# Cross-attention and mixture-of-experts kernel: VectorE subtracts the score maxima of two of four units, and every engine's calls stand in a new order

## The reference

```python
x = x + xattn(layernorm(x), ctx, ctx)     # 8 heads of width 16
x = x + moe(layernorm(x))                 # 8 experts, top 2, hidden width 256
# xattn: q, k, v = projections; scores = q k^T / 4
#        attn = softmax(scores, axis=1)   # axis 1 is the HEAD axis
#        out = (attn v) W_O
# moe:   gates = softmax of the two largest router logits, 0 elsewhere
#        out = sum_e gates_e * (relu(x W1_e + b1_e) W2_e + b2_e)
```

## Time and profile before

| | |
|---|---|
| median of three runs | 210.16 us |
| span of the profiled execution | 207.8 us |
| instructions | 4986 |
| TensorE, VectorE busy | 199.5 us, 167.8 us |
| ScalarE, GpSimd busy | 132.2 us, 112.3 us |

### The profile page before, as it was taken

The page is one execution under the profiler, slowest core; times in us unless marked ns, Lnnn a source line. Parts: engine busy times, 40 slices in busy tenths (PEclk is TensorE's granted clock), DMA queues, the critical chain, the costliest instruction groups (busy, mean ns, idle before and its releaser), DMA issues.

```text
span 207.8 us, 4986 instructions
## 1 busy us (share of the span) xinstructions
PE 199.5 (96%) x1752; PEld 176.5 (85%) x1752; DVE 167.8 (81%) x453; ACT 132.2 (64%) x316; POOL 112.3 (54%) x132
## 2 busy tenths in 40 slices
PE   6999988798999999999999999999999999999995
PEld 6845976686799979997999799998998899789994
DVE  6398769889789999899788988898999888556633
ACT  2236748697568847797677767677757776345441
POOL 8502647869976378629561966376746674010000
PEclk9999999999999999999999999999999999999999
DMA  6649595716515133423140504241000000000000
GB/s 175 160 127 286 153 279 148 224 46 183 158 62 145 69 108 106 103 76 104 41 147 25 170 3 151 57 144 36 0 0 28 0 2 3 25 3 2 25 3 25
DMA packets 20264, 18.70 MB, mean 90 GB/s; under 512 B 1776, under 2 KB 18704, under 8 KB 20240
## 3 DMA queue, kind: packets, MB, share of 16 engines
q1 hardware_dynamic: 17344, 16.85, 28.0%
q10 hardware_dynamic: 2896, 1.54, 2.8%
HBM read 11.83 MB, written 6.55 MB: 88 GB/s over the span
## 4 chain that ended last, share of the span: by engine, by line
PE 91%; DVE 3%; ACT 2%; issue 1%; POOL 1%; POOLq 0%; ACTq 0%; DVEq 0%
PE y_ps L436 28%; PE h_ps L421 22%; PE score_ps L361 7%; PE misc_ps L380 6%; PE score_ps L349 6%; PE h_ps L369 4%; PE score_ps L277 3%; PE misc_ps L401 2%; PE score_ps L338 2%; PE score_ps L421 2%; PE misc_ps L389 2%; PE misc_ps L287 1%; PE misc_ps L327 1%; PE misc_ps L306 1%; PE misc_ps L300 1%
## 5 line engine op out<-in xcount | busy, mean ns | idle before, releaser
L695 ACT ACTIVATE hT<-h_ps,b_sb 128x256 f32<-128x256 f32 x118 | 49.4, 470 | 33.3 <-PE h_ps L421 32.1
L436 PE MATMUL y_ps<-w_sb,hT 128*128 128x128 f32 x508 | 68.0, 277 | 0.0
L436 PEld LDWEIGHTS y_ps<-w_sb,hT 128*128 128x128 f32 x508 | 62.8, 191 | 3.5 <-issue 2.2
L1188 POOL TENSOR_TENSOR half_sum<-e_sb 128x512 f32<-128x512 f32 x28 | 37.3, 1332 | 30.8 <-ACT e_sb L667 30.5
L938 DVE TENSOR_TENSOR attn<-e_sb,e_rcp 128x1024 f32<-128x1024 f32 x32 | 42.1, 1319 | 3.3 <-ACT e_rcp L678 3.3
L930 DVE TENSOR_REDUCE shift_m<-score_ps 128x128 fp32r<-128x1024 f32 x32 | 38.7, 1212 | 2.2 <-PE score_ps L338 1.1
L421 PE MATMUL h_ps<-x1T_hi,w_lo 128*128 128x256 f32 x118 | 37.7, 320 | 1.5 <-ACT hT L695 0.9
L667 ACT ACTIVATE e_sb<-score_ps 128x1024 f32<-128x1024 f32 x32 | 32.8, 1024 | 5.6 <-PE score_ps L361 5.4
L1007 DVE SCALAR_TENSOR_TENSOR acc<-y_ps,gates,acc 128x128 f32<-128x128 f32 x96 | 29.0, 342 | 8.6 <-PE y_ps L436 7.3
L421 PE MATMUL h_ps<-x1T_hi,w_hi 128*128 128x256 f32 x118 | 33.1, 280 | 0.0
L421 PE MATMUL h_ps<-x1T_lo,w_hi 128*128 128x256 f32 x118 | 33.1, 280 | 0.0
(11 more groups left out here) (117 smaller groups left out, 291.3 us busy)
## 6 DMA issues: line engine op xcount, KB each, us to landing
k_scratch<-k_parts SPq DMA_DIRECT2D x14, 256.0 KB, 2.6
k_stack<-k_scratch SPq DMA_DIRECT2D x14, 256.0 KB, 4.0
q_stack<-q_scratch SPq DMA_DIRECT2D x28, 128.0 KB, 2.7
q_scratch<-q_parts SPq DMA_DIRECT2D x7, 256.0 KB, 2.7
w_sb<-in_w SPq DMA_DIRECT2D x1, 1024.0 KB, 6.6
out_y<-y_out SPq DMA_DIRECT2D x7, 128.0 KB, 1.9
x_all<-in_x ACTq DMA_DIRECT2D x1, 768.0 KB, 6.2
ctxT<-in_ctx_t SPq DMA_DIRECT2D x1, 640.0 KB, 6.1
```

Source lines behind the costliest of these rows:

```text
L436: mm = nc.tensor.matmul(product(j, t), hT[:, j % 2, c, t * P:(t + 1) * P], w2_sb[:, e * HC + c, :], start=(c == 0), stop=(c == HC - 1))
L695: op = nc.scalar.activation(hT[:, j % 2, c, :], hidden(j)[:, c * S:(c + 1) * S], ACT.Relu, bias=b1_sb[:, e * HC + c:e * HC + c + 1])
L1188: nc.gpsimd.tensor_tensor(half_sum[:], e[:, 0:HQ // 2], e[:, HQ // 2:HQ], ALU.add).then_inc(sum_step, 1)
```

## The change

From batch 1 on, units 2 and 3 are no longer shifted on TensorE. Behind its maximum VectorE subtracts it from the scores, from PSUM into `e_sb`, and ScalarE takes the exponential of `e_sb` in place. The scores' bank is still released by the exponential. All periods are unrolled, and each engine has one list of calls in an order of its own. The diff is cut here to the new step and to the parts of the order that the prediction speaks of.

```diff
+    VECTOR_UNITS = (2,3,)
+    FIRST_VECTOR = 1
...
+        def vector_shifts(n):
+            return n >= UNITS * FIRST_VECTOR and n % UNITS in VECTOR_UNITS
+
+        def shifts_on_vector(n):
+            return sum(vector_shifts(k) for k in range(n))
...
             def subtract_max(b, u):
+                if vector_shifts(UNITS * b + u):
+                    return
...
             def exponentiate(b, u):
                 n = UNITS * b + u
-                act.wait_ge(shifted, n + 1)
+                if vector_shifts(n):
+                    act.wait_ge(vector_shifted, shifts_on_vector(n + 1))
+                    nc.scalar.activation(e_sb[:, u, :], e_sb[:, u, :], ACT.Exp, scale=SCALE).then_inc(exp_made, 1)
+                    return
+                act.wait_ge(shifted, n + 1 - shifts_on_vector(n))
...
             def head_max(b, u):
...
+                n = UNITS * b + u
+                if vector_shifts(n):
+                    dve.wait_ge(max_made, n + 1)
+                    wait(dve, attn_made, n - 3)
+                    nc.vector.tensor_tensor(e_sb[:, u, :].rearrange("p (h q) -> p h q", h=H),
+                                            score_ps[:, u % 2, :].rearrange("p (h q) -> p h q", h=H),
+                                            shift_m[:, u % 2, :].bitcast(F32).unsqueeze(1).to_broadcast([P, H, P]),
+                                            ALU.subtract).then_inc(vector_shifted, 1)
```

The start of SyncE's queue, as calls. Before: `x(0)`, `ctxT(0)`, `spill_k(1)`, `load w1`, `load_k_stack(1)`, `spill_q(1)`, `load_q_stack(1)`, `spill_k(2)`, `load ctxT(3..7)`, `load_k_stack(2)`, `spill_q(2)`, `load_q_stack(2)`, `load w2`. After:

```diff
+            load_first()
+            load_w1()
             spill_k(1)
             load_k_stack(1)
+            load_ctx_rest()
             spill_q(1)
+            spill_k(2)
+            spill_q(2)
+            load_k_stack(2)
+            load_w2()
+            load_q_stack(2)
             load_q_stack(1)
```

On ScalarE's queue the loads were w_qkvo, x(1), ctxT(1), ctxT(2), the rest of x, the small ones, and then `take_k_first`. After:

```diff
+            load_w_qkvo()
+            load_tables()
+            load_x1()
+            load_ctx(2)
+            load_small()
+            take_k_first()
+            load_ctx(1)
+            take_xnT(0)
+            take_k_hi(1)
+            load_x_rest()
+            split_w1(0)
+            split_w1(1)
+            exponentiate(0, 0)
+            exponentiate(0, 1)
+            take_k_hi(2)
+            invert_sum(0, 0)
+            take_xnT(1)
+            make_xn(2)
+            make_xn(3)
+            invert_sum(0, 1)
+            take_q_hi(1)
+            take_xnT(2)
+            exponentiate(0, 2)
+            exponentiate(0, 3)
+            invert_sum(0, 2)
+            take_q_hi(2)
```

TensorE's start after (before, `project_v(0)` stood second, `project_q(0)` ahead of `project_k(1)`, `project_q(1)` ahead of `subtract_max(0, 1)`, and head sums and scores of batch 1 alternated):

```diff
+            keep_warm(12)
+            project_k(0, None, 0)
+            keep_warm(5)
+            transpose_xn(0, None, 0)
+            keep_warm(1)
+            project_k(1, k_first_made, 1)
+            keep_warm(2)
+            project_q(0, xnT_taken, 1)
+            first_scores(0)
+            first_scores(1)
+            project_k(2, None, 0)
+            transpose_xn(1, q_wide_made, 2)
+            subtract_max(0, 0)
+            head_sum(0, 0, k_lo_made, 1)
+            subtract_max(0, 1)
+            first_scores(2)
+            first_scores(3)
+            head_sum(0, 1, log_made, 1)
+            subtract_max(0, 2)
+            project_q(1, xnT_taken, 2)
+            subtract_max(0, 3)
+            transpose_xn(2, k_lo_made, 2)
+            head_sum(0, 2, log_made, 2)
+            project_q(2, xnT_taken, 3)
+            scores(1, 0)
+            scores(1, 1)
+            project_v(0, None, 0)
+            head_sum(0, 3, log_made, 3)
+            attend_values(0, q_lo_made, 2)
```

VectorE's start after:

```diff
             ln1(0, TT, 0)
             ln1_end(0, 0)
+            ln1(2, 4, 1)
+            negate_ident()
+            k_lo(1)
+            mark_heads()
+            split_wr()
+            spread_q(0)
+            spread_q(1)
+            head_max(0, 0)
+            head_max(0, 1)
+            ln1_end(1, 1)
+            ln1(4, 6, 2)
+            ln1(6, 10, 3)
+            head_max(0, 2)
+            head_max(0, 3)
+            k_lo(2)
+            normalize(0, 0)
+            normalize(0, 1)
+            q_lo(1)
+            ln1(10, 16, 4)
+            normalize(0, 2)
+            q_lo(2)
+            head_max(1, 0)
+            head_max(1, 1)
+            normalize(0, 3)
+            add_residual(0)
```

More of the change, by code:

```diff
@@ L441, in expert_down @@
                     mm.then_inc(y_done, 1)
[L443 to L503, removed]
@@ new lines, in _ @@
+            route(0, x1T_lo_made, 1)
+            expert_up(0, 0)
+            scores(2, 0)
+            expert_up(0, 1)
+            subtract_max(1, 3)
+            expert_up(0, 2)
+            expert_down(0, 0)
+            project_k(3, logits_made, 1)
+            scores(2, 1)
+            subtract_max(2, 0)
+            expert_down(0, 1)
+            transpose_xn(3, k_lo_made, 3)
+            expert_up(0, 3)
+            expert_down(0, 2)
+            project_q(3, xnT_taken, 4)
+            expert_up(0, 4)
@@ new lines, in _ @@
+            subtract_max(2, 1)
+            scores(2, 2)
+            attend_values(1, q_lo_made, 3)
+            gated_b2(0, heads_taken, 2)
+            scores(2, 3)
+            subtract_max(2, 2)
+            expert_up(0, 5)
+            expert_down(0, 3)
+            project_out(1, b2_added, 1)
+            expert_up(0, 6)
+            project_k(4, x1_made, 2)
+            expert_down(0, 4)
+            expert_down(0, 5)
+            transpose_x1n(1, k_lo_made, 4)
+            scores(3, 0)
@@ new lines, in _ @@
+            subtract_max(2, 3)
+            expert_down(0, 6)
+            expert_up(0, 7)
+            route(1, x1T_lo_made, 2)
+            expert_up(1, 0)
+            expert_down(0, 7)
+            transpose_xn(4, logits_made, 2)
+            expert_up(1, 1)
+            project_v(3, xnT_taken, 5)
+            scores(3, 1)
+            subtract_max(3, 0)
+            project_q(4, v_taken, 4)
+            expert_up(1, 2)
+            expert_down(1, 0)
+            project_v(4, q_lo_made, 4)
@@ new lines, in _ @@
+            subtract_max(3, 1)
+            scores(3, 2)
+            attend_values(2, v_taken, 5)
+            expert_up(1, 3)
+            project_out(2, heads_taken, 3)
+            expert_down(1, 1)
+            expert_down(1, 2)
+            scores(3, 3)
+            expert_up(1, 4)
+            project_k(5, x1_made, 3)
+            subtract_max(3, 2)
+            expert_down(1, 3)
+            expert_up(1, 5)
+            gated_b2(1, k_lo_made, 5)
+            expert_down(1, 4)
+            transpose_xn(5, b2_added, 2)
@@ new lines, in _ @@
+            expert_up(1, 6)
+            subtract_max(3, 3)
+            scores(4, 0)
+            transpose_x1n(2, xnT_taken, 6)
+            expert_down(1, 5)
+            expert_up(1, 7)
+            subtract_max(4, 0)
+            route(2, x1T_lo_made, 3)
+            expert_down(1, 6)
+            scores(4, 1)
+            expert_up(2, 0)
+            project_q(5, logits_made, 3)
+            expert_down(1, 7)
+            scores(4, 2)
+            subtract_max(4, 1)
+            project_v(5, q_lo_made, 5)
@@ new lines, in _ @@
+            subtract_max(5, 1)
+            project_v(6, q_lo_made, 6)
+            expert_up(3, 2)
+            attend_values(4, v_taken, 7)
+            expert_down(3, 1)
+            project_out(4, heads_taken, 5)
+            scores(5, 2)
+            subtract_max(5, 2)
+            expert_up(3, 3)
+            project_k(7, x1_made, 5)
+            expert_down(3, 2)
+            scores(5, 3)
+            expert_up(3, 4)
+            gated_b2(3, k_lo_made, 7)
+            expert_down(3, 3)
+            expert_up(3, 5)
@@ new lines, in _ @@
+            expert_down(4, 0)
+            project_v(7, q_lo_made, 7)
+            expert_up(4, 2)
+            scores(6, 2)
+            attend_values(5, v_taken, 8)
+            subtract_max(6, 1)
+            expert_up(4, 3)
+            expert_down(4, 1)
+            subtract_max(6, 2)
+            scores(6, 3)
+            expert_down(4, 2)
+            expert_up(4, 4)
+            project_out(5, heads_taken, 6)
+            expert_down(4, 3)
+            expert_down(4, 4)
+            expert_up(4, 5)
```

1136 lines of the change are left out of this document (658 added, 478 removed).

## The result

The changed kernel takes **339.53 us** (median of 4 runs, 336.51 to 342.87), the kernel before 209.83 us on the same chip (4 runs, 209.46 to 210.30). The ratio is 1.6139, with a 95% interval of 1.6051 to 1.6227. The forecast was 240 us, with a range of 226 to 248: the sign was right, and the loss is 129.7 us where some 30 were foreseen. The longest run, 342.87, counts as a slow one, and the ratio is that of the fast runs; the other three have a median of 338.42.

The account below looks back on a forecast made before the run. TensorE bounds the old kernel, VectorE the new middle. Residual at 52.4 + 147.8 work + 4 waits = 204.2; + 0.1 + 30.9 + 2.1 = span 237.3; with 2.4 from span to median, 240 us, range 226 to 248.

Parts of the forecast that it names:

- The bound of the kernel before: Steady middle: TensorE sets the pace, busy all 22.00 us per batch; VectorE 19.17, under 3 us to spare.
- the price of the subtraction: VectorE, 14 subtractions at the median 1.22 us: 17.1 us added, ends 16.5 and 24.6.
- The start: Up to batch 0's residual: late load_q_stack(1) puts scores(1, 0) at 44.0, add_residual(0) at 52.4 against 34.56.
- both estimates: Stack of batch 1: 2.8 MB from 33.4 at 312 GB/s, or issue times plus landing; both give 43 to 45.
- The landings: DMA at the start: a q_stack piece takes 2.7 us to land.
- the clock rival: TensorE at half pace for 24 matmuls after the start's idle stretch: 2.5 us more, 242.5 us, chance 0.2.
- The middle: Batch 0's residual to normalize(7, 3): VectorE work 147.8 us plus 4 of waits, from 52.4 to 204.2.
- the rivals: Clock, 242.5 us, chance 0.2; start costs little, 222, 0.12; faster, 204, 0.03; no change, 210, 0.02.
- The end: After normalize(7, 3): attend_values(7) to last output 30.9 us, with four more expert calls, then 2.1 for the store.
- ScalarE's side: Exponentials stay at 1.02 us; reading SBUF in place of PSUM costs nothing, ScalarE being busy 64%.

Follow-up runs that it names:

- all moves made: Changed kernel with SyncE's old list, plus normalize(b, 3) earlier, attend_values(2) to (7) later and the start's calls put back: 282.27 us.

## Why the prediction was wrong, step by step

**The bound of the kernel before, and the price of the subtraction: right.** 14 x 1.22 = 17.1 us was forecast and 14 x 1.224 = 17.1 measured. With nothing but the subtraction changed, the middle took 150.95 us, against 131.9 + 17.1 + 4 = 153.0 by the prediction's sum, and 4.0 us of named waits were left, the very 4 that it allowed. That 5.0 of the lost 7 us fall on one batch it did not have.

**The start: right in mechanism, short in size.** The forecast had load_q_stack(1) last, issued at 38 to 41, and scores(1, 0) at 44.0. The trace has q_lo(2) ending at 35.25 (33.3 forecast), SyncE's whole series 2 us late with it, and both q_stacks issued back to back in 5.34 us; the scores ran at 49.01, against 43 to 45 from both estimates. The landings were the term that was sized too small: the eight q_stack pieces took 5.5 us each from issue to landing (median), not 2.7, and from 36 to 49 us the core moved 222 GB/s, not 312. The 2.6 us for the load of ctxT, taken from no row, was 3.6, and the load was issued 0.8 us earlier than forecast, so that the two errors nearly cancel by luck. From there to the residual the forecast allowed 8.4 us, and it took 12.2: the head sum took 2.75 us instead of 1.98 and attend_values 3.39 instead of 1.86. The mean granted clock from 40 to 60 was 0.59 of full speed, mostly the 1.2 GHz level, after an idle stretch. This was the clock rival, held at 2.5 us. The Trainium skill ("TensorE: Matmul & The Clock Gate", Part 1) has an idle array fall back from 2.4 to 1.2 GHz; by that rule the trace agrees, with 0.51 from 36 to 49 us, where TensorE ran no matmul. And it did so again behind later stalls, not once as the rival assumed (attend_values(7) took 3.64 us after 3.2 us of waiting). Together the start is 8.8 us over the forecast. The late stack is not the whole delay of the residual, 61.17 - 34.56 = 26.6 us: with SyncE's old list and the new computing lists the residual came at 51.43, and with SyncE's new list and the old computing lists at 52.16.

**The middle: the step that failed.** The prediction said "Waits cannot vanish. I leave 4 of the 11.8 us, as TensorE is no longer full", and ended the middle at 204.2. In its place came 86.3 us in which VectorE is idle (with the small gaps between its instructions), and normalize(7, 3) ended at 289.8. Of the 97.3 us that the forecast of the span missed (334.6 in place of 237.3), 76.9 arose here (228.73 in place of 151.8), 8.8 in the start and 11.6 in the end. The step summed the work in each queue and took the sum for the time. A sum is right only if the queue is never empty-handed, and the order decides that. The runs name these places:
- stacks queued on SyncE behind the next batch's keys: 22 us behind the start, 26 to 37 with the start's part of the list;
- the computing engines' order between the residuals of batches 0 and 3, which is part of the 19 us above;
- normalize(b, 3) behind the next batch's maximum on VectorE: 13.7 us;
- attend_values directly behind its own producers on TensorE: 9.6 us;
- of the other 34 us or so of the four engines' new order behind the start (57.8 - 13.7 - 9.6), no run shows the places. With all moves made, the waits between expert_down and add_expert are the largest row left on TensorE (22.2 us over the whole span), but no kernel moved them, so that they are the cause is only argued.

The prediction's own test, "If VectorE idles over 12 us in the middle, it is not the bound, and the order is", came true. But such an order had been given no chance and no price among the rivals: they varied the start, the clock and the dose, and all of them kept a saturated middle.

**The end: 44.7 us for a forecast of 33.1** from the last normalisation to the end of the span. attend_values(7) took 3.64 us in place of 1.86:

```profile
286.64 3.23 issue
289.88 3.64 PE misc_ps L422 x32
293.52 1.58 PE h_ps L463 x6
295.10 1.26 PE y_ps L478 x8
```

The rest of it is busy TensorE only in part (35.27 of 44.70 us). The calls that the prediction counted are all there; again their sum was a lower bound.

**ScalarE's side was right**: an exponential from SBUF took 1.05 us after 1.02 from PSUM, and its busy time is 131.7 us after 132.2.

## What to carry to other kernels

Work per engine, summed, gives the time of a reordered kernel only from below. Before believing the sum, walk one batch of the new lists through all queues, the DMA queue included, and write down for every wait the call that ends it and what stands ahead of that call on *its* engine; a consumer placed directly behind its producer, or a wanted load behind the next batch's, is a stall of several microseconds in each batch. Where stalls are forecast, price TensorE's lower clock after each of them, and test an addition to one engine in the old order first: here that separated 7 us from 130.

## What the runs showed that was not expected

- TensorE was busy 23.9 us longer with 28 instructions fewer. Busy time of TensorE is not an amount of work where the granted clock varies: the same 32 passes of attend_values took 1.86 or 3.64 us.
- Filling a wait with matmuls did not help when they began after a wait and outlasted it: 40 passes in 4.70 us, on the chain.
- The subtraction in the old order lost 5.0 of its 7 us in one batch, and 0.3 us in each of two steady ones, though VectorE then has 2.2 us more work in each.
- Gains of moves on three engines added up, 30.9 us for 32.1 (single runs), even though all work on the same loop of queues.
- Small VectorE operations of the start were slower in one order than in the other: two 128x128 subtractions with scale (ln1_end) took 1.87 us here and 0.60 before, with a GpSimd operation beside them here. No run isolates that.
